# A third PSUM bank for the last two expert passes, half of the second layer's last window inside the last pass, and its modulations on VectorE

## The reference

```
h = layernorm(x)*(1+ca)+sa ; x += ga * deltanet(h)            # layer 0: gated delta rule, 16 heads of 8
h = layernorm(x)*(1+cb)+sb ; x += gb * (h + sum_e w_e*expert_e(h))   # 8 experts, top 2 as weights
h = layernorm(x)*(1+ca)+sa ; x += ga * ssd(h)                 # layer 1: chunks of 64 tokens
h = layernorm(x)*(1+cb)+sb ; x += gb * butterfly_ffn(h)       # 128 -> 512 -> 128, gelu
```

## Time and profile before

| | |
|---|---|
| time, median of 3 runs | 488.26 us (487.59 to 488.83) |
| time of the profiled execution | 488.68 us |
| its span | 486.1 us |
| mean granted TensorE clock | 0.979 |
| PE / DVE / ACT / POOL busy | 426.6 / 343.3 / 363.9 / 165.6 us |

### The profile page before, as it was taken

One profiled execution on the slowest core, in us unless ns is written; L12 is line 12 of the kernel. 1 busy time (PEld: TensorE's weight loads), 2 busy tenths in 40 slices (PEclk: granted clock), 3 DMA queues, 4 the chain that ended last, 5 costly groups with the idle time before them and its releaser, 6 DMA issues. The chain is left out here.

```text
span 486.1 us, 7168 instructions
## 1 busy us (share of the span) xinstructions
PE 426.6 (88%) x2168; PEld 312.2 (64%) x2168; DVE 343.3 (71%) x876; ACT 363.9 (75%) x643; POOL 165.6 (34%) x236
## 2 busy tenths in 40 slices
PE   3498797869998699999999999999999878999666
PEld 2395674547776576757676656776676646798434
DVE  1545988877899984999999899998434681212751
ACT  4849688876985669889669794849988888646544
POOL 1060860684165963365940173161200001000010
PEclk9859999889999999999999999999999999999999
DMA  7999635012830228300204801000001000000000
GB/s 194 315 365 252 221 87 122 2 50 66 224 79 0 55 50 216 99 0 13 76 1 114 213 6 23 1 1 0 2 0 24 0 1 1 23 1 1 0 0 22
DMA packets 34484, 35.46 MB, mean 73 GB/s; under 512 B 12808, under 2 KB 30608, under 8 KB 34192
## 3 DMA queue, kind: packets, MB, share of 16 engines
q1 hardware_dynamic: 34016, 30.77, 23.9%
q10 hardware_dynamic: 432, 4.26, 2.3%
HBM read 13.78 MB, written 1.05 MB: 31 GB/s over the span
## 5 line engine op out<-in xcount | busy, mean ns | idle before, releaser
L874 PEld LDWEIGHTS psS<-we2s,hid 128*128 128x128 f32 x1024 | 130.5, 193 | 33.2 <-issue 29.5
L859 PE MATMUL psF<-h,we1s 128*128 128x256 f32 (+1 forms) x384 | 135.7, 461 | 9.0 <-ACT hid L1649 8.3
L874 PE MATMUL psS<-we2s,hid 128*128 128x128 f32 x1024 | 131.8, 277 | 5.5 <-DVE acc L2296 5.5
L1649 ACT ACTIVATE hid<-psF,col 128x256 f32<-128x256 f32 (+1 forms) x192 | 99.2, 542 | 48.4 <-PE psF L859 42.9
L859 PEld LDWEIGHTS psF<-h,we1s 128*128 128x128 f32 x384 | 65.6, 192 | 43.9 <-issue 21.6
L3309 POOL TENSOR_TENSOR QS<-H,qn 128x256 f32<-128x256 f32 x64 | 52.5, 834 | 96.8 <-DVE H L2282 74.7
L2296 DVE SCALAR_TENSOR_TENSOR acc<-psS,gate,acc 128x128 f32<-128x128 f32 x128 | 40.6, 342 | 44.4 <-PE psS L874 44.0
L2282 DVE TENSOR_TENSOR_SCAN H<-A,psT 128x320 f32<-128x320 f32 x64 | 52.1, 814 | 1.2
L2254 DVE TENSOR_TENSOR psT<-wrep,H 128x360 f32<-128x360 f32 x63 | 42.9, 681 | 10.4 <-DMA wrep<-XX 8.6
L1449 ACT ACT_TABLE_LOAD x37 | 47.5, 1283 | 1.8 <-PEq L3614 1.2
L3360 POOL TENSOR_TENSOR x<-x,gdb 128x512 f32<-128x512 f32 (+1 forms) x5 | 4.4, 870 | 130.0 <-PE psM L690 129.0
(11 more groups left out here) (264 smaller groups left out, 656.3 us busy)
## 6 DMA issues: line engine op xcount, KB each, us to landing
wrep<-XX SPq DMA_DIRECT2D x72, 160.0 KB, 3.4
krep<-kn SPq DMA_DIRECT2D x64, 128.0 KB, 2.5
hid<-fold_mats_dram SPq DMA_DIRECT2D x22, 256.0 KB, 4.4
we1s<-we_dram ACTq DMA_DIRECT2D x1, 2048.0 KB, 7.9
we2s<-we_dram ACTq DMA_DIRECT2D x1, 2048.0 KB, 13.7
outT_dram<-x SPq DMA_DIRECT2D x3, 256.0 KB, 2.6
M<-mats_dram SPq DMA_DIRECT2D x1, 576.0 KB, 4.3
x<-xT_dram SPq DMA_DIRECT2D x2, 256.0 KB, 7.1
```

The lines of the kernel that those rows point to most:

```text
L859: mm(bank[name][:, 0:(b - a) * TWS[w]], we1s[:, e, k * P:(k + 1) * P], h2[w % 2][:, a * TWS[w]:b * TWS[w]], start=True, stop=True).then_in ...
L874: last = mm(bank[name][:, t * P:(t + 1) * P], hid[n % 2][:, k, t * P:(t + 1) * P], we2s[:, e, k, :], start=(k == 0), stop=(k == HT - 1))
L1649: nc.scalar.activation(hid[x_ % 2][:, k, 0:c], psF[n % 2][:, 0:c], ACT.Silu, bias=pc("be1", HT * e + k)).then_inc(s_hid_done, 1)
```

## The change

Three edits, and an order written anew for every engine.

- In passes 4 and 5 (from LATE on) the hidden layer's quarters rotate over F0, F1 and `psT`. From the third quarter of pass 4 on PE waits once for the last scan.
- `modulate` of units 3 and 4 ("ssd" and "ffn", four calls) is on VectorE, as 4 TENSOR_SCALAR of 128x64 each.
- Unit 3's ssd part, from `variance` to `ssd_residual`, stands inside pass 5 on all engines; its ffn part stays behind it.

```diff
+LATE = len(EU) - 2
+        def hid_bank(u, e, k):
+            n = HT * (EXPERTS * (u - LATE) + e) + k
+            return f"F{n % 2}" if u < LATE else ("F0", "F1", "T")[n % 3]
...
             def first(u, e, k):
-                name = f"F{n % 2}"
+                name = hid_bank(u, e, k)
+                if u == LATE and e == 0 and k == 2:
+                    pe.wait_ge(s_scan_done, SEQ // CH)
...
-                nc.scalar.activation(hid[x_ % 2][:, k, 0:c], psF[n % 2][:, 0:c], ACT.Silu,
+                nc.scalar.activation(hid[x_ % 2][:, k, 0:c], bank[hid_bank(u, e, k)][:, 0:c], ACT.Silu,
...
             def modulate(key):          # VectorE
+                if key not in WIDE:
+                    for i, b in enumerate(ln_batches(key)):
+                        last = v_.tensor_scalar(out[:, i, :], out[:, i, :], mod[:, 6 * l + c, b:b + 1], mod[:, 6 * l + s, b:b + 1],
+                                                ALU.mult, ALU.add)
+                    last.then_inc(s_ln_h, 1)
+                    return
...
             projected(0, 4)             # ScalarE
-            load_weights()
             norms(0)
+            folded(0)
             inverse_norms(0)
-            folded(0)
...
-            for i in range(9, 16):
+            for i in range(9, 15):
                 folded(i)
+            load_weights()
+            folded(15)
```

More of the change, by code:

```diff
@@ L1315, in _ @@
             second(4, 1, 1)
-            ssd_steps(2)
-            ssd_in(2)
             first(4, 3, 0)
@@ L1379, in _ @@
             first(5, 4, 0)
             first(5, 4, 1)
-            center(("ssd", 3))
+            ssd_in(3)
             second(5, 3, 0)
             first(5, 4, 2)
+            second(5, 3, 1)
             first(5, 4, 3)
-            second(5, 3, 1)
-            first(5, 5, 0)
-            first(5, 5, 1)
+            for i in range(0, 4):
+                first(5, 5, i)
             second(5, 4, 0)
-            first(5, 5, 2)
-            first(5, 5, 3)
+            first(5, 6, 0)
+            ssd_conv(3)
@@ L2028, in _ @@
             ln_scale(("ffn", 2))
-            hidden(4, 7, 0)
-            hidden(4, 7, 1)
+            for i in range(0, 4):
+                hidden(4, 7, i)
             modulate(("ffn", 2))
-            hidden(4, 7, 2)
-            hidden(4, 7, 3)
             for i in range(0, 4):
@@ L2065, in _ @@
             ssd_shifted(3)
+            for i in range(0, 4):
+                hidden(5, 6, i)
+            ssd_norm(3)
+            for i in range(0, 4):
+                hidden(5, 7, i)
+            ln_square(("ssd", 4))
+            ln_scale(("ssd", 4))
+            ssd_in(4)
+            ssd_steps(4)
             ssd_gate(4)
-            ssd_in(4)
+            ln_square(("ffn", 3))
             ssd_decay(4)
             ssd_shifted(4)
-            ssd_norm(3)
+            ln_scale(("ffn", 3))
             ssd_norm(4)
-            ln_square(("ffn", 3))
-            ln_scale(("ffn", 3))
-            ln_square(("ffn", 4))
-            modulate(("ffn", 3))
-            ln_scale(("ffn", 4))
             ffn_act(3, 0)
             ffn_act(3, 1)
-            modulate(("ffn", 4))
+            ln_square(("ffn", 4))
+            ln_scale(("ffn", 4))
             ffn_act(3, 2)
@@ L2885, in _ @@
             chunk_scan(3, 10)
+            mix(2, 2, 1)
             chunk_seed(3, 11)
@@ L3169, in _ @@
             ssd_shift(3)
+            mix(5, 4, 0)
+            mix(5, 4, 1)
+            ssd_input(3)
+            ssd_weights(3)
+            ssd_values(3)
+            ssd_norms(3)
+            ssd_total(3)
+            ssd_norm(3)
+            mix(5, 5, 0)
+            mix(5, 5, 1)
+            mix(5, 6, 0)
+            ssd_residual(3)
+            mix(5, 6, 1)
+            mix(5, 7, 0)
+            mix(5, 7, 1)
+            experts_residual(5)
+            ln(("ssd", 4))
+            modulate(("ssd", 4))
             ssd_sum(4)
@@ L3537, in _ @@
+            read_state(4, 15)
             attn_gate(7)
```

1320 lines of the change are left out of this document (646 added, 674 removed).

## The result

The changed kernel takes 498.38 us (median of 4 runs, 493.05 to 498.52) against 488.54 (487.59 to 488.89): 1.0153 times as long, 95% interval 1.0111 to 1.0194. Predicted were 480.2 us, between 476.2 and 485.5. In a later comparison of 12 runs the same kernel took 495.01 (489.95 to 498.92), ratio 1.0089, interval 1.0058 to 1.0120. So it is slower by 0.9 to 1.5%, and its own executions lie 9 us apart.

The account below looks back on a forecast made before the run. Bound: a start where PE lacks work, a long PE-bound part, a chained end. 488.68 - 1.0 - 1.0 - 2.4 + 3.6 - 7.3 = 480.6, less 0.42 for the profiled execution: 480.2 us, 8 in 10 range 476.2 to 485.5.

Parts of the forecast that it names:

- The step that failed: Between 115 and 372 us, outside the other terms: reordering PE's own work costs 0, as PE is full there.
- One sign of being wrong: The forecast is wrong if PE's full stretch starts later than in the kernel before.
- The start and window 2: Start: folding products before small ones, -1.0; window 2: earlier square sums and scan shorten DVE's 3.00 wait, -1.0.
- the recurrence comes late: Windows 2 and 3: later convolution silu delays keys and solved rows 5 us each, full stretch 10 later; 492.2, chance 0.05.
- The end: Behind pass 5: without unit 3's ssd part, 38.2 us becomes 30.9, -7.3; bounds 4.0 to 8.5.
- The walk: Unit 4's chain behind pass 5, step by step on the old clock: first scan at 456.4, residual 465.4, `ffn_up` 470.1.
- Pass 5: Unit 3's ssd part inside: 3.0 us of PE products plus 0.6 of waits, +3.6; bounds +3.0 and +9.
- the named sign: In pass 5 PE's waits on `hid` total less than 1 us.
- Pass 4: Third bank lets quarters go ahead at five PE waits, 1.5 us, with the filler -2.4; bounds 0 and 6.6.
- The sign "less than 5 us of waits": In pass 4 PE's waits, 5.69 us before, come to fewer than 5 us.

Follow-up runs that it names:

- the new order of it alone in a fast kernel: The late-only kernel with PE, ACT and DVE in the changed order from the ("moe", 2) to the ("moe", 3) centre product: 488.94 us, ratio 1.0002.
- the old order behind a late start: The changed kernel with PE, ACT and DVE back in the order of before from pass 1 on, two banks and old end: 495.95 us, ratio 1.0115.
- the head alone: The kernel before with the changed order on all engines only up to window 1's first hidden quarters (about 81 us): 489.70 us, ratio 1.0024.
- late-only: The kernel before with the changed order, third bank and DVE modulations only from unit 2's ssd layer norm in pass 4 on: 485.83 us, again 485.90.
- early part: Changed order up to unit 2's ssd layer norm in pass 4; alone, with the kernel before's order behind it, 496.83 us, ratio 1.0181.

## Why the prediction was wrong

**The step that failed** is the sentence "All else between 115 and 372 is PE's own work in another order: 0, as it is full there". PE is full only as long as the recurrence on DVE stays ahead of it. I took PE's busy share as proof that another order can't cost; it is proof only for the order that was profiled. The new order lets DVE wait 11.5 instead of 7.4 us between ("moe", 2) and ("moe", 3), window 3's scans take 4.1 longer, and PE waits for them. That the stretch costs is shown by the new order of it alone in a fast kernel (+3.8 in it, +3.0 in all) and by the old order behind a late start (69.39 us). That DVE's waits are the reason is read from the traces: in the fast kernel they grow from 7.2 to 10.3 us. One sign of being wrong that I had named, that PE's full stretch starts later than now, did come.

**The start and window 2**, -2.0 in the sum, were +5.9 in the profiled execution, and -0.5 to +5.9 against the one profile of before over all nine with this order (by the medians of the traces +2.4). PE's pause of 6.13 became 3.76 and the small products take 2.30 instead of 4.28, yet DVE's coupling starts at 34.63, where it did, and the head alone is +1.1 and not -1.0. For window 2 I weighed the silu of the convolution, which comes 4.96 later on ScalarE (88.60 for 83.64). That cost nothing: the squares behind it start at 90.33, at 90.32 before. In the profiled execution PE fell to the lower level between its own waits at 88 and 90 us, and where it falls differs from one execution to the next. I had seen half clock near 33 us and not asked where else it falls. But the clock is not the whole answer: at 2.4 GHz all through that stretch (1.00 from 82 to 105 us) 2.2 us were lost all the same. The cause of the rest stays open.

**The rival that came near**, "the recurrence comes late" at 492.2, had 0.05. Its 5 us per window come near the +5.9 and +5.1 of the first profile by luck, for its mechanism is another: DVE's wait for transferred rows in the second stretch fell from 2.0 to 1.2 us, so it was not keys and solved rows that landed late, but what was put between the chunks. I argued against it with the earlier square sums, one moved pair where hundreds of calls moved.

**The end**: 32.5 for 30.9, a gain of 5.7 instead of 7.3. Over the twelve traces with this end and DVE's modulations it is 31.9 to 34.2 us long, so the 32.5 of the first profile is among the shortest. The walk was right up to the first scan: 8.7 us behind pass 5, where 8.5 was forecast. From there to the end of unit 4's residual it is 9.5 for 9.0, and from that to its `ffn_up` 5.5 for 4.7, with unit 3's `ffn_up` ahead of unit 4's centre on the chain (480.29 and 482.04) and 0.13 more for the modulation. The convolution at 1.2 GHz (3.4 us) is hardly part of it: DVE's input product waits 0.20 for it, and the late-only trace has it in 1.97 and the end in 33.1.

**Pass 5**: 2.6 more for 3.6 forecast (2.8 from unit 2's last ffn product on). PE's waits on `hid` are 0.19 and 0.36, as the named sign had it.

**Pass 4**: -2.4 forecast. It is +0.7 in the changed kernel and -0.7 in the late-only one. The waits are still there: 2.41, 0.71, 1.35, 1.31 and 0.16, 5.9 for 5.69. My reading is that a third bank lets PE run one quarter further ahead, and that the new order spends this by asking for ScalarE's modulation sooner; no run separates the two. The sign "less than 5 us of waits" was not met.

## What to carry to other kernels

A full engine shows that the profiled order keeps it fed, not that any order would; before an edit of the order is put down as 0, the engine that feeds it has to be walked, wait by wait. An edit that helps should be moved alone: here the same late part is worth -3 us on the old order, and is lost in the +8 us and more of an early part that was written anew along with it. When parts of two orders are put together the seam can cost more than the part, so read the waits at the seam before reading the total.

## What the runs showed of the hardware

- The executions of one program lie 9 us apart (489.95 to 498.92), and those of the kernel before in the same comparison 5.3 (488.17 to 493.46), with the mean granted clock of PE going the other way (there 0.979 at the fast end and 0.965 at the slow one).
- 16 inert products put into PE's waits gave 1.6 us of 486 in the late-only kernel, with the mean granted clock at 0.979 and more instead of 0.961 to 0.972. In the changed kernel, with four or eight, no gain can be told from its scatter.
- A table load takes 1.28 us, and the next activation starts 0.01 to 0.02 us behind its end (466.23, then 467.52; 482.94, then 484.24).
- Four TENSOR_SCALAR of 128x64 with two scalars per partition take 0.98 us on DVE, four SCALAR_TENSOR_TENSOR of the same size, which read a tensor more, 0.86.
